# Shared expert of a mixture-of-experts layer in units of four tiles, and a new order between attention and expert blocks

## What is computed

```
def _swiglu(xt, wu, wg, wd):
    return jax.nn.silu(xt @ wu.T) * (xt @ wg.T) @ wd.T
...
probs = jax.nn.softmax(logits, axis=-1)
topk_weight, topk_idx = jax.lax.top_k(probs, TOPK)
...
for e in range(E):
    y = y + combine[:, e:e + 1] * _swiglu(xt, w1[e], w3[e], w2[e])
y = y + _swiglu(xt, sw1, sw3, sw2)
...
x = x + jnp.tanh(g_xattn[0]) * _L0_xattn_ref(_layernorm(x, axis=-1), ctx_1024, ...)
x = x + jnp.tanh(g_ffn[0]) * _L0_ffn_ref(_layernorm(x, axis=-1), ...)
```

## Time and profile before

| | us |
|---|---|
| median of 3 runs | 243.32 (242.53 to 243.35) |
| profiled execution | 242.78 |
| its span, first to last instruction | 241.0 |
| TensorE busy in the span | 218.7 (91%) |
| VectorE busy | 151.2 (63%) |
| GpSimd busy | 130.8 (54%) |
| ScalarE busy | 119.7 (50%) |
| TensorE's granted clock, mean | 0.990 |

### The profile page before, as it was taken

The page is one execution under the profiler, slowest core; times in us unless marked ns, Lnnn a source line. Parts: engine busy times, 40 slices in busy tenths (PEclk is TensorE's granted clock), DMA queues, the critical chain, the costliest instruction groups (busy, mean ns, idle before and its releaser), DMA issues.

```text
span 241.0 us, 4750 instructions
## 1 busy us (share of the span) xinstructions
PE 218.7 (91%) x1490; PEld 187.2 (78%) x1490; DVE 151.2 (63%) x333; ACT 119.7 (50%) x244; POOL 130.8 (54%) x121
## 2 busy tenths in 40 slices
PE   3899999998999999977888999999999999999940
PEld 1777767786999989975776879888898889888930
DVE  0399979999887989776979695263343334234310
ACT  3377768729755566564724523444334443444220
POOL 4225222363859999857648934446554556454222
PEclk9999999999999999999999999999999999999995
DMA  6934438021221444223013401322243224322322
GB/s 194 303 109 152 170 117 272 36 65 65 65 90 67 152 155 152 88 68 109 22 44 91 131 24 22 66 47 46 45 65 69 44 46 62 68 47 24 36 32 23
DMA packets 12775, 20.99 MB, mean 87 GB/s; under 512 B 2032, under 2 KB 7664, under 8 KB 12752
## 3 DMA queue, kind: packets, MB, share of 16 engines
q1 hardware_dynamic: 9104, 15.71, 20.0%
q0 software_dynamic: 3648, 4.98, 12.7%
HBM read 16.10 MB, written 4.59 MB: 86 GB/s over the span
## 4 chain that ended last, share of the span: by engine, by line
PE 70%; DVE 11%; DMA 10%; issue 4%; ACT 2%; POOLq 1%; SPq 1%; ACTq 0%; DVEq 0%
PE bankQ L242 6%; DMA out_dram<-probs,tok 6%; PE bankQ L244 6%; PE bankQ L243 6%; PE bankP L242 6%; PE bankR L358 5%; PE bankP L244 5%; PE bankP L243 5%; PE bankS L242 5%; PE bankS L243 5%; PE bankS L244 5%; DMA raw<-kvq_dram 4%; PE bankR L554 3%; DVE spot L1107 2%; PE bankR L405 2%
## 5 line engine op out<-in xcount | busy, mean ns | idle before, releaser
L1441 POOL DMA_INDIRECT out_dram<-probs,tok x19 | 30.1, 1584 | 46.2 <-ACT probs L812 25.0
L1413 POOL TENSOR_TENSOR reg<-raw,reg 128x768 fp32r<-128x768 f32 x16 | 29.5, 1846 | 4.6 <-ACT reg L766 4.4
L1432 POOL DMA_INDIRECT probs<-x2d,tok x19 | 20.5, 1079 | 9.0 <-issue 8.1
L1381 POOL TENSOR_TENSOR w_lo<-raw,w_hi 128x512 fp32r<-128x512 f32 x8 | 10.4, 1298 | 24.0 <-ACT w_hi L690 24.0
L242 PE MATMUL bankS<-reg,hT 128*128 x76 | 21.6, 284 | 1.9 <-DVE hT L1214 1.9
L1214 DVE TENSOR_TENSOR hT<-bankR,hT 128x512 fp32r<-128x512 f32 x19 | 13.1, 691 | 15.2 <-ACT hT L796 15.2
L812 ACT ACTIVATE probs<-bankS,wgt_tab 128x256 f32<-128x256 f32 x14 | 6.6, 474 | 32.1 <-DMA out_dram<-probs,tok 24.8
L243 PE MATMUL bankS<-reg,hT 128*128 x76 | 21.6, 284 | 0.0
L244 PE MATMUL bankS<-reg,hT 128*128 x76 | 21.5, 283 | 0.0
L1205 DVE TENSOR_TENSOR gT_lo<-bankS,gT_hi 128x256 fp32r<-128x256 f32 x19 | 8.0, 423 | 21.4 <-ACT gT_hi L786 21.4
L1394 POOL TENSOR_TENSOR probs<-probs,rcp 128x1024 f32<-128x1024 f32 x8 | 15.2, 1906 | 5.8 <-DVE rcp L1007 5.7
(11 more groups left out here) (232 smaller groups left out, 693.9 us busy)
## 6 DMA issues: line engine op xcount, KB each, us to landing
raw<-ffn_dram SPq DMA_DIRECT2D x18, 384.0 KB, 3.3
raw<-kvq_dram SPq DMA_DIRECT2D x7, 384.0 KB, 3.5
probs<-wo_dram SPq DMA_DIRECT2D x8, 256.0 KB, 2.7
x_sb<-x_dram SPq DMA_DIRECT2D x1, 1024.0 KB, 6.0
x2d<-xn SPq DMA_DIRECT2D x8, 128.0 KB, 1.7
...
probs<-x2d,tok POOLq DMA_INDIRECT x19, 2.9
out_dram<-probs,tok POOLq DMA_INDIRECT x19, 3.8
```

Source lines behind the costliest of these rows:

```text
L1381: pool.tensor_tensor(w_lo[:, s, 0:2 * D], raw_kvq[:, s, 2 * HD:KVQ], w_hi[:, s, 0:2 * D].bitcast(F32), ALU.subtract).then_inc(wq_lo, 1)
L1413: pool.tensor_tensor(lo, raw[:, (m + 2) % RS, :], hi.bitcast(F32), ALU.subtract).then_inc(wf_lo, 1)
L1432: pool.indirect_dma_start(out=x_blk[:, i % 4, :], out_offset=None, in_=x2d[:, :], in_offset=bass.IndirectOffsetOnAxis(ap=tok[:, i:i + 1], ...
L1441: pool.indirect_dma_start(out=out[:, :], out_offset=bass.IndirectOffsetOnAxis(ap=tok[:, i:i + 1], axis=0), in_=y_blk[:, i % 4, :], in_offs ...
```

## The change

The shared expert works in four units u instead of eight tiles: u = 2*half + j stands for four tiles of tokens (512) and 128 of the 256 hidden units. In `shared_up(u, mat)` 128 x 128 of the weights are the stationary side and 512 tokens the moving side, once for the silu matrix (mat 0) and once for the gate (mat 1). The hidden values so come out with hidden units on partitions, as `shared_down` needs them: `shared_turn` goes. `shared_silu`, `shared_gate` and `shared_split` work on 512 columns, and the split's source is SBUF instead of PSUM. `shared_down(n)` stays per tile, with its sums alternating between two places in PSUM; `add_shared(n)` is now VectorE's and reads PSUM, so ScalarE's `shared_out` and GpSimd's `add_shared` go. `below_largest` is a part of `choose` as a function of its own. The rest is order: gate_logits(4) and turn_x2(5) stand in the last attention tile, the table load for silu comes after split_x2(5), GpSimd gathers without sums between, `weigh(0)` moves into block 0, one `spots` into block 1, `token_table(1)` behind the up projection of block 2, tokens_of(5) behind out_block(1). Cut to its core (bodies that only change an index, and routing counters, are left out; old bodies stand above):

```diff
@@ -160,10 +160,9 @@
...
-        s_y = over("s_y", SP2 + 2560, [P, 2, D], F32)
-        sT_hi = over("sT_hi", SP2 + 3072, [P, 2, HS], F32R)
...
+        sT = [over("sT_first", SP3, [P, 2, JS, 4 * P], F32R), over("sT_rest", SP2 + 2048, [P, 2, JS, 4 * P], F32R)]
@@ -189,10 +189,12 @@
...
-        su_ps = [bankP[:, 0, :], bankP[:, 1, :]]
-        sh_ps, sd_ps = bankQ[:, 0, 0:HS], bankQ[:, 1, 0:D]
+        su_ps = [(bankP[:, 0, :], bankP[:, 1, :]), (bankQ[:, 0, :], bankR[:, 0, :])]
...
+        sd_ps = [bankQ[:, 1, 0:D], y_acc]
@@ -429,9 +431,12 @@
...
-                wait(pe, lg_rd, n)
+                if n == NT - 2:
+                    pe.wait_ge(x1_ok, NT)
+                else:
+                    wait(pe, lg_rd, min(n, NT - 2))
...
-                    mm = pe.transpose(turn_ps[:, k * P:(k + 1) * P], xn2[:, n % 2, k * P:(k + 1) * P], ident[:, :])
+                    mm = pe.transpose(x2t_ps[n][:, k * P:(k + 1) * P], xn2[:, n % 2, k * P:(k + 1) * P], ident[:, :])
@@ -439,36 +444,32 @@
...
-            def shared_up(n):
...
+            def shared_up(u, mat):
...
+                hf, j = divmod(u, JS)
+                t = slice(hf * 4 * P, (hf + 1) * 4 * P)
+                pe.wait_ge(x2_lo, 4 * hf + 4)
+                wait(pe, s_gate, u - 1)
...
+                    c = slice((mat * KD + k) * P, (mat * KD + k + 1) * P)
+                    mm = split3(pe, su_ps[j][mat], w_hi[:, j, c], w_lo[:, j, c], xT_hi[:, k, t], xT_lo[:, k, t], k == 0, k == KD - 1)
...
-            def shared_turn(n):
...
+            def shared_down(n):
...
+                hf = n // 4
+                pe.wait_ge(s_lo, JS * (hf + 1))
+                wait(pe, xf_ok, n - 1)
+                if n == 0:
+                    pe.wait_ge(settled, 1)
+                if n == 1:
+                    pe.wait_ge(lg_rd, NT - 1)
...
-            def shared_down(n):
...
+                    mm = split3(pe, sd_ps[n % 2], sT[hf][:, 0, j, cols(n % 4)], sT[hf][:, 1, j, cols(n % 4)],
+                                w_hi[:, j, UPC:FFC], w_lo[:, j, UPC:FFC], j == 0, j == JS - 1)
@@ -617,56 +618,45 @@
...
             turn_p(7, 1)
+            gate_logits(4)
             attend(7, 0)
-            gate_logits(4)
+            turn_x2(5)
             attend(7, 1)
-            turn_x2(5)
...
             pe.wait_ge(wf_lo, JS)
-            pe.wait_ge(x1_ok, NT - 2)
-            shared_up(0)
+            pe.wait_ge(x1_ok, NT - 1)
+            shared_up(0, 0)
             places(0)
+            shared_up(0, 1)
             gate_logits(5)
-            pe.wait_ge(x1_ok, NT - 1)
-            shared_up(1)
             turn_x2(6)
-            shared_turn(0)
-            shared_up(2)
+            pe.wait_ge(pt_lo, 2 * NT)
+            shared_up(1, 0)
+            turn_x2(7)
+            shared_up(1, 1)
             gate_logits(6)
-            shared_turn(1)
-            pe.wait_ge(settled, 1)
-            shared_down(0)
-            shared_up(3)
-            turn_x2(7)
-            shared_turn(2)
-            shared_down(1)
+            shared_up(2, 0)
+            shared_up(2, 1)
             gate_logits(7)
             token_table(0)
-            shared_up(4)
-            shared_turn(3)
+            shared_down(0)
+            shared_down(1)
+            shared_up(3, 0)
+            shared_up(3, 1)
             shared_down(2)
-            shared_up(5)
-            shared_turn(4)
             shared_down(3)
-            shared_up(6)
-            shared_turn(5)
+            e = [expert_of(0)]
             shared_down(4)
-            shared_up(7)
-            shared_turn(6)
             shared_down(5)
-            e = [expert_of(0)]
+            shared_down(6)
             turn_block(0)
-            shared_turn(7)
-            shared_down(6)
             pe.wait_ge(wf_lo, NM)
...
                 if i == 1:
-                    pe.wait_ge(s_out, NT)
-                if i == 2:
-                    token_table(1)
+                    pe.wait_ge(xf_ok, NT)
                 up_block(i, e[i], lambda: turn_hidden(i - 1) if i > 0 else shared_down(7))
@@ -674,6 +664,8 @@
...
                     weight_table(0)
+                if i == 2:
+                    token_table(1)
                 if i > 0:
@@ -765,20 +757,16 @@
...
-            def shared_silu(n):
...
-            def shared_split(n):
...
-            def shared_out(n):
...
+            def shared_silu(u):
+                act.wait_ge(s_up, 2 * u + 1)
+                if u == 0:
+                    act.wait_ge(pv_ps, NT)
+                wait(act, s_lo, u - 1)
+                act.activation(s_hid[:, u % 2, :], su_ps[u % JS][0], ACT.Silu).then_inc(s_silu, 1)
...
+            def shared_split(u):
+                act.wait_ge(s_gate, u + 1)
+                act.copy(sT[u // JS][:, 0, u % JS, :], s_hid[:, u % 2, :]).then_inc(s_hi, 1)
@@ -787,11 +775,15 @@
...
+                if i == 0:
+                    act.wait_ge(s_lo, 2 * JS)
...
+                if i == 0:
+                    act.wait_ge(s_dn, NT)
@@ -879,54 +871,47 @@
...
             split_p(7, 1)
+            normal_x2(5)
+            split_w(14)
+            split_x2(5)
             act.wait_ge(lsub_ok, 1)
...
             act.activation(warm[:, :], mhalf[:, 0:1], ACT.Silu)
-            normal_x2(5)
-            split_w(14)
-            split_x2(5)
+            normal_x2(6)
             shared_silu(0)
             split_w(15)
-            normal_x2(6)
-
-            shared_silu(1)
+            split_w(16)
+            normal_x2(7)
             split_x2(6)
             shared_split(0)
-            normal_x2(7)
+            split_x2(7)
+            shared_silu(1)
+            split_w(17)
+            shared_split(1)
             shared_silu(2)
-            shared_split(1)
-            split_w(16)
-            shared_out(0)
+            shared_split(2)
+            c = [tokens_of(0)]
             shared_silu(3)
-            split_x2(7)
-            shared_split(2)
-            split_w(17)
-            c = []
-            for n in range(4, NT):
-                shared_out(n - 3)
-                shared_silu(n)
-                shared_split(n - 1)
-                for i in range(max(2 * n - 9, 0), min(2 * n - 7, FIRST)):
-                    c.append(tokens_of(i))
-            shared_out(NT - 3)
+            c.append(tokens_of(1))
+            shared_split(3)
+            for i in range(2, FIRST - 1):
+                c.append(tokens_of(i))
             split_block(0)
-            shared_split(NT - 1)
-            shared_out(NT - 2)
+            c.append(tokens_of(FIRST - 1))
...
                     split_hidden(i - 1)
-                if i > 1 and i + FIRST - 1 - (i == 2) < NBLK:
-                    c.append(tokens_of(i + FIRST - 1 - (i == 2)))
-                if i == 0:
-                    shared_out(NT - 1)
+                if i > 2 and i + FIRST - 1 < NBLK:
+                    c.append(tokens_of(i + FIRST - 1))
                 silu_block(i)
...
                 if i == 2:
+                    c.append(tokens_of(FIRST))
                     c.append(tokens_of(FIRST + 1))
@@ -1040,24 +1025,39 @@
...
-            def shared_gate(n):
...
-            def shared_split(n):
...
+            def shared_gate(u):
+                dve.wait_ge(s_silu, u + 1)
+                dve.wait_ge(s_up, 2 * u + 2)
+                dve.tensor_tensor(s_hid[:, u % 2, :], su_ps[u % JS][1], s_hid[:, u % 2, :], ALU.mult).then_inc(s_gate, 1)
...
+            def shared_split(u):
+                dve.wait_ge(s_hi, u + 1)
+                dve.tensor_tensor(sT[u // JS][:, 1, u % JS, :], s_hid[:, u % 2, :],
+                                  sT[u // JS][:, 0, u % JS, :].bitcast(F32), ALU.subtract).then_inc(s_lo, 1)
...
+            def add_shared(n):
+                dve.wait_ge(s_dn, n + 1)
+                dve.scalar_tensor_tensor(xtile(n), sd_ps[n % 2], tg[:, 1:2], xtile(n), ALU.mult, ALU.add).then_inc(xf_ok, 1)
...
+            def below_largest(h):
+                t0, t1 = GROUPS[h]
+                lg = logits[:, t0:t1, :]
+                dve.wait_ge(lg_rd, t1)
+                dve.tensor_reduce(lmax[:, t0:t1], lg, AX.X, ALU.max).then_inc(largest, 1)
+                dve.wait_ge(largest, h + 1)
+                dve.tensor_tensor(lsub[:, t0:t1, :], lg, lmax[:, t0:t1].unsqueeze(2).to_broadcast([P, t1 - t0, NE]),
+                                  ALU.subtract).then_inc(lsub_ok, 1)
...
+                k, nt = h * 9, t1 - t0
@@ -1310,63 +1306,62 @@
...
             add_attention(6)
+            statistics(6)
             split_p(7, 1)
+            aggregate(6)
+            read_logits(4)
+            below_largest(0)
             choose(0)
-            read_logits(4)
-            statistics(6)
-            aggregate(6)
-            settle(0)
             split_x2(5)
...
-
-            shared_gate(0)
+            settle(0)
             spots(0, 0, 2)
             read_logits(5)
+            shared_gate(0)
+            split_x2(6)
+            spots(0, 2, 4)
+            split_x2(7)
```

(50 more changed lines are left out.)

72 lines of the change are left out of this document (19 added, 53 removed).

## The result

The changed kernel takes 240.78 us (median of 20 runs, 239.73 to 242.75) against 243.03 (20 runs, 241.34 to 244.49) of the kernel before in the same measurement: a ratio of 0.9932, 95% interval 0.9906 to 0.9958. That is 2.25 us by the medians; the ratio says less, 0.7% or 1.7 us (its interval 1.0 to 2.3 us). The 20 executions of the changed kernel fall into two groups, 14 from 239.73 to 241.19 and six from 242.12 to 242.75, and the median lies in the lower one. The forecast was 239.4 out of 243.32, a gain of 3.9 us. The profiled execution took 240.14, with a span of 238.4 against 241.0.

The account below looks back on a forecast made before the run. TensorE was taken to bound the kernel, with 5.9 us idle between attention's end and the first expert block. Block 0 5.5 us earlier, less 1.7 lost in the first blocks, gave -3.8 us: 239.4 from 243.32, range 237.0 to 241.9.

Parts of the forecast that it names:

- TensorE's own work: Between attention's end and block 0: TensorE's pieces after the change sum to 20.3 us, some 1.5 us saved by dropped transposes.
- The wait of 1.52: TensorE's wait for ScalarE's normalised tile 5, ahead of turn_x2(5): claimed to go, with attend(7,1) covering it.
- Start of block 0: First expert block's first up matmul: claimed at 129.5 instead of 134.98, 5.5 us earlier, bounds 6.7 and 3.7.
- VectorE's list: VectorE's order ahead of block 0: choose(0) as before, settle(0) over at 109.1, 1.5 us earlier, sel done at 118.5.
- the walk: Four engines followed through the new order with the profile's durations, up to block 0's start at 129.5.
- The other holds: VectorE's spots, shared_split(0) and hit ahead of block 0: each waits once for a GpSimd weight split.
- Rival (b): GpSimd holds VectorE up for one more weight split of 1.84 on the path: gain 2.0, 241.4; chance 0.16.
- First blocks: VectorE's added work in block 0 delays the split of hidden 0 and down_block(0): loss 1.2 to 2.1, taken 1.7 us.
- Gather 5: tokens_of(5) behind out_block(1): gather lands as turn_block(5) asks; worth 0 to 0.3, with the largest landing 2.0; taken as 0.
- Scatters: Scatters start up to 1.9 us later behind gather 5, but catch up by block 12; taken as 0.
- The sum: Whole kernel: -5.5 ahead of block 0 plus 1.7 in the first blocks, -3.8 us.

Follow-up runs that it names:

- u1: Changed kernel with ScalarE's exponent and silu table load ahead of normal_x2(5) again, TensorE's turn_x2(5) behind attend(7,1) again: 241.13 us, ratio 0.9935.
- e1: Changed kernel with choose(0)'s product rest*from_end (tiles 0 to 3) issued after aggregate(7), directly ahead of settle(0): 239.53 us, ratio 0.9865 to the kernel before.
- e3: Changed kernel with GpSimd making the low parts of the last four weight tiles on only 16 of 768 columns: 237.99 us, ratio 0.9798 to the kernel before.
- e6: Changed kernel with spots(1,4,6) moved from block 0 to block 1: 240.62 us, ratio 0.9884 to the kernel before.
- e10: Changed kernel with rest*from_end after aggregate(7), turn_block(0) ahead of shared_down(6), split_block(0) ahead of add_shared(6), weigh(0) directly ahead of add_shared(7): 237.19 us, ratio 0.9766.
- e5: Changed kernel with tokens_of(5) ahead of out_block(1) again: 241.48 us, ratio 0.991 to the kernel before.
- a0: The changed kernel run once more, unedited: 240.98 us, ratio 0.994 to the kernel before.

## Why the prediction was wrong

The direction and the place were right; the time is within the range (237.0 to 241.9), but the gain is 1.7 us by the ratio and 2.25 by the medians where 3.9 was forecast. Two errors of opposite sign partly cancel, and that part is luck: block 0 came 1.1 us too late, the first blocks lost 0.6 us less than priced.

- **TensorE's own work, right.** 20.3 us forecast, 20.29 busy in the stretch. That fits a sum in which the units of four tiles bring the transposes' time and nothing else; no run has the units without the new order, so their share is not shown separately.
- **The wait of 1.52 goes, right.** There is none at turn_x2(5); undone in u1 it is 1.12.
- **Start of block 0, wrong: -5.5 forecast, -4.4 measured** (from the last turn_p). The step that failed is the start of VectorE's list, which put no hold there: "choose(0) as before", "settle(0) is over at 109.1". VectorE's own order was followed through, but not what the new order on ScalarE does to GpSimd: it gets its half of weight tile 14 earlier, beside the product, which I priced as 0.17 and which took 1.85. settle(0) so ended at 110.4, and TensorE waited 0.60 for tile 7's normalised rows, a wait that the walk did not have. e1 takes just this product out and gives 26.9 where the forecast had 27.0. The Trainium skill, SBUF — State Buffer, section Who interferes with whom, says whole blocking between a VectorE instruction with two SBUF inputs and a GpSimd one that reads SBUF. The runs agree (1.85 beside a split of 1.85; 0.42 with one input in PSUM; 0.17 in u1 beside nothing, 0.22 in e3 beside a split of 16 columns that took 0.22 itself). I had weighed the rule for the large instructions alone; an instruction of 16 columns is held just as long.
- **The other holds, right in kind.** Expected were three (spot, shared_split(0), hit); spot took 1.61, shared_split(0) 1.98, hit 1.25, and TensorE waited 0.41, 0.85 and 0.80 where 0.3, 1.0 and 0.5 to 0.7 were forecast. Rival (b), one more weight split on the path, gave 241.4 at a chance of 0.16 and is in mechanism what happened, at 1.2 us instead of 1.84: the product took 1.7 more, and e1 shows that block 0 starts 1.2 earlier without it.
- **First blocks, right in kind, too large: +1.7 forecast, +1.07 measured.** choose(1) and split_block(1) were behind add_shared(7) as said (wait 0.28 of turn_block(2)), and the split of hidden 0 was late by weigh(0) and a spot (wait 0.95, forecast about 1.5). VectorE's timeline of after has the list behind gate_block(0):

```profile
135.39 0.16 DVE L1093 TENSOR_TENSOR place<-bankR,rest 128x16 int32<-128x16 f32 x1
...
135.75 0.16 DVE L1121 TENSOR_REDUCE lsum<-lexp 128x4 f32<-128x16 f32 x1
...
137.95 1.22 DVE L1103 TENSOR_TENSOR spot<-iota_j,slot 128x1024 bf16<-128x1024 f32 x1
139.09 0.42 DVE L1201 TENSOR_TENSOR gT_lo<-bankS,gT_hi 128x256 fp32r<-128x256 f32 x1
139.42 0.68 DVE L1210 TENSOR_TENSOR hT<-bankR,hT 128x512 fp32r<-128x512 f32 x1
```

From start to start settle takes 0.36, weigh 2.20, the spot 1.14, where 0.5, 2.4 and 1.17 were forecast, and the list began at +4.7, not +4.9 to +5.5. The split of hidden 0 so ended at +9.45, under the forecast's +9.9 to +10.5, and down_block(0) began at +9.59. e6 and e10 show that this pile is the cause: with one spot or weigh(0) elsewhere the 1.1 us are gone.
- **Gather 5, nearly right:** 0.2 measured by e5 (0 to 0.3 forecast, taken as 0).
- **Scatters, nearly right.** From the seventh on they start 4.85 us apart, like the blocks, sooner than the forecast's block 12. The end of the table, last turn_block to last scatter, is 16.3 us after and 15.8 before; the last gap between scatters is 5.27 against 4.63. The other profiles range from 15.9 to 17.9 without order, a0 with the same kernel has 15.9, so nothing is to be read from it for this change. The forecast had no such spread in its sum.
- **The sum.** Against the forecast's -3.8, block 0 brought 1.1 less (the product, 1.2 by e1), the first blocks cost 0.6 less, and three things that the sum had at nothing cost 0.8: blocks 3 to 18 0.2, the end 0.5, attention 0.1. That makes -2.6 in the profiles (rounded terms). Each profile is one execution; the spread of where attention ends (2.2 us over the profiles) and of the last scatters (2 us) is larger than what separates 2.6 from 2.25 and 1.7, and that was not separated further.
